# The roll layer's last four images in two groups of two, without filler products

## The reference

```python
def _L1_attn_ref(x, W_A, W_V, W_O, b_O):
    z = jnp.einsum('bse,he->bsh', x, W_A) * SCALING
    z = jax.nn.softmax(z, axis=1)
    zp = jnp.transpose(z, (0, 2, 1))
    ...
    idx = (i - j) % S
    tril = (j <= i).astype(x.dtype)
    roll = zp[:, :, idx] * tril
    v = jnp.einsum('bse,fe->bsf', x, W_V).reshape(B, S, H, D)
    out = jnp.einsum('bhij,bjhd->bihd', roll, v).reshape(B, S, E)
    return jnp.einsum('bse,fe->bsf', out, W_O) + b_O
...
h = h + _L1_attn_ref(_layernorm(h, axis=-1), ...)
h = h + _L1_ffn_ref(_layernorm(h, axis=-1), ...)
```

## Time and profile before

| What | Value |
|---|---|
| median of 3 runs | 1072.96 us (1072.81 to 1073.27) |
| the profiled execution | 1074.8 us, its span 1073.0 us |
| mean granted TensorE clock over the span | 0.936 |
| PE busy | 939.0 us, 88% of the span |
| DVE, ACT, POOL busy | 582.3, 412.1, 519.4 us |
| roll layer, its steps 7 and 8 | from 806.4 to 850.8 us, 22.2 us each |
| roll layer, its steps 9 and 10 | from 850.8 us to DVE's last instruction at 874.8 us |

### The profile page before, as it was taken

The page is one execution under the profiler, slowest core; times in us unless marked ns, Lnnn a source line. Parts: engine busy times, 40 slices in busy tenths (PEclk is TensorE's granted clock), DMA queues, the critical chain, the costliest instruction groups (busy, mean ns, idle before and its releaser), DMA issues. The chain is left out here.

```text
span 1073.0 us, 29482 instructions
## 1 busy us (share of the span) xinstructions
PE 939.0 (88%) x10318; PEld 741.5 (69%) x10318; DVE 582.3 (54%) x1439; ACT 412.1 (38%) x1094; POOL 519.4 (48%) x714
## 2 busy tenths in 40 slices
PE   8699999978824999999999986599999954999996
PEld 6457777767722888888888875255665634888895
DVE  1768888855995677533333325678877432111111
ACT  2357667743334343443434311233333222333331
POOL 0045565620603777777677617777772002343332
PEclk9879999979967999999999989789999976999998
DMA  7010000002003988887888723335463047466750
GB/s 253 2 44 2 0 0 0 1 2 84 1 0 109 307 267 271 279 243 214 254 261 253 231 80 103 103 104 140 122 214 125 21 153 261 138 224 236 282 154 25
DMA packets 79820, 149.28 MB, mean 139 GB/s; under 512 B 18892, under 2 KB 53327, under 8 KB 75760
## 3 DMA queue, kind: packets, MB, share of 16 engines
q1 hardware_dynamic: 34768, 77.15, 21.4%
q0 software_dynamic: 17712, 47.88, 15.7%
q10 hardware_dynamic: 27248, 23.09, 6.4%
HBM read 200.22 MB, written 31.73 MB: 216 GB/s over the span
## 5 line engine op out<-in xcount | busy, mean ns | idle before, releaser
L1311 POOL DMA_INDIRECT x_x<-m_x_rows,x_idx x170 | 165.8, 975 | 75.2 <-issue 35.9
L1337 PE MATMUL x_pup<-x_xt,x_w 128*128 128x128 f32 (+1 forms) x2176 | 184.7, 251 | 0.0
L1337 PEld LDWEIGHTS x_pup<-x_xt,x_w 128*128 128x128 f32 (+1 forms) x2176 | 168.7, 166 | 6.0 <-issue 5.9
L1606 POOL DMA_INDIRECT rl_y<-m_y_rows,rl_idx x136 | 132.8, 976 | 46.3 <-issue 36.9
L1407 DVE TENSOR_TENSOR x_hid<-x_gate,x_pup 128x128 f32<-128x128 f32 x170 | 48.9, 288 | 148.3 <-ACT x_gate L1379 144.3
L1351 PE MATMUL x_pdown<-x_w,x_hid 128*128 128x256 f32 (+1 forms) x408 | 104.2, 389 | 0.3 <-DVE x_y L1414 0.3
L1375 ACT ACTIVATE x_xt<-x_pturn 128x256 f32<-128x256 f32 x170 | 65.3, 384 | 88.9 <-PE x_pturn L1322 86.0
L434 POOL TENSOR_TENSOR wa_probs<-wa_probs,wa_peak 68x544 f32<-68x544 f32 x64 | 69.9, 1092 | 58.7 <-DVE wa_peak L576 58.7
L2365 DVE TENSOR_TENSOR x_y<-x_pdown,x_b 128x256 f32<-128x256 f32 x21 | 8.9, 425 | 151.3 <-PE x_pdown L2321 151.3
L2351 ACT ACTIVATE x_hid<-x_pup,x_b 128x128 f32<-128x128 f32 (+1 forms) x200 | 52.9, 356 | 93.3 <-PE x_pup L2304 93.1
L1379 ACT ACTIVATE x_gate<-x_pup 128x128 f32<-128x128 f32 x170 | 47.2, 278 | 93.5 <-PE x_pup L1337 92.8
(11 more groups left out here) (329 smaller groups left out, 1886.8 us busy)
## 6 DMA issues: line engine op xcount, KB each, us to landing
x_w<-in_experts SPq DMA_DIRECT2D x204, 384.0 KB
late_w<-in_w SPq DMA_DIRECT2D x28, 1024.0 KB, 14.5
m_y_rows<-x_y ACTq DMA_DIRECT2D x170, 128.0 KB
xT<-in_w SPq DMA_DIRECT2D x12, 1024.0 KB, 6.2
xn<-in_w SPq DMA_DIRECT2D x10, 1024.0 KB, 10.7
h<-in_w SPq DMA_DIRECT2D x10, 1024.0 KB, 14.7
m_x_rows<-xn SPq DMA_DIRECT2D x34, 128.0 KB, 1.9
x_x<-m_x_rows,x_idx POOLq DMA_INDIRECT x170, 3.1
```

The costliest lines, as they stand in the source:

```text
L1311: nc.gpsimd.indirect_dma_start(x[:, s, :], None, x_rows, bass.IndirectOffsetOnAxis(ap=idx[:, s:s + 1], axis=0))\
L1337: mm = nc.tensor.matmul(pup[rows:rows + wide, bank, m * P + side * wide:m * P + (side + 1) * wide], w[:, lane, first:first + wide], xt[:, ...
L1606: nc.gpsimd.indirect_dma_start(y[:, t % YR, kk, :], None, y_rows, bass.IndirectOffsetOnAxis(ap=idx[:, n:n + 1], axis=0))\
```

## The change

The list `SIZES` replaces the constant number of groups: seven groups of four images and two of two. The pipeline has one step more (12 instead of 11). Tile 15 becomes the end of group 7 and tile 16 that of group 8; the out part of group 6 has tiles 12 and 13, that of group 7 tile 14, that of group 8 tiles 15 and 16. No group projects more than two tiles any more, so `project` and `add_projected` run once a group. The instructions of a group of two have half the columns or half the count. The three filler helpers return at once, without their waits, for groups 7 and 8 (the last two, as g1 in steps 8 and 9). The fillers of the closing branch stay: eight ahead of the inverse, and three behind it. Since NG is now 9, SP's four weight loads stand ahead of the rows of group 5 instead of group 4.

```diff
-    NG = B // GI
+    GI, PAIR = 4, 2
+    SIZES = [4] * 7 + [2] * 2
+    NG = len(SIZES)
+    FROM = [sum(SIZES[:g]) for g in range(NG + 1)]
...
-        return list(range(0 if g == 0 else 2 * g + 1, 2 * g + 3))
+        return list(range(-(-FROM[g] * S // P), -(-FROM[g + 1] * S // P)))
...
-        return list(range(2 * g, NT if g == NG - 1 else 2 * g + 2))
...
+        return list(range(FROM[g] * S // P, FROM[g + 1] * S // P))
+
+    def halves(g):
+        return range(SIZES[g] // PAIR)
...
-                        mm = nc.tensor.matmul(pz[0:H, 0:GC], late["w_a"][:, c, :], xT[:, c, g * GC:(g + 1) * GC],
+                        mm = nc.tensor.matmul(pz[0:H, 0:SIZES[g] * S], late["w_a"][:, c, :], xT[:, c, cols_of(g)],
...
                 def fill(g, n):
+                    if NG - 2 <= g < NG:
+                        return
...
                 def fill_values(g, n):
-                    pe.wait_ge(v_moved, g * 2 + 2)
+                    if NG - 2 <= g < NG:
+                        return
+                    pe.wait_ge(v_moved, pairs_through(g))
...
                 def fill_mid(g, n):
-                    if not 0 <= g < NG:
+                    if not 0 <= g < NG - 2:
                         return fill(g, n)
...
                         fill(g2 + 1, 8)
-                        invert(g2, 0)
-                        fill(g2 + 1, 4)
-                        invert(g2, 1)
-                        fill(g2 + 1, 2)
-                        for m, ts in pairs_out(g2):
-                            project(g2, m, ts)
+                        for p in halves(g2):
+                            invert(g2, p)
+                            fill(g2 + 1, 3)
+                        project(g2)
...
                     if has1:
-                        values(g1, 1)
+                        for p in halves(g1)[1:]:
+                            values(g1, p)
```

More of the change, by code:

```diff
@@ L1476, in roll_layer @@
     inv = [k["const"]("inv_re"), k["const"]("inv_neg"), k["const"]("inv_im"), k["const"]("inv_im")]
-    GI = 4
-    NG = B // GI
+    GI, PAIR = 4, 2
+    SIZES = [4] * 7 + [2] * 2
+    assert sum(SIZES) == B
+    NG = len(SIZES)
+    FROM = [sum(SIZES[:g]) for g in range(NG + 1)]
     GC = GI * S
-    CP = 2 * S
+    CP = PAIR * S
     YR = 4
@@ L1490, in tiles_out, with pair_of, pairs_through, cols_of @@
             return []
-        return list(range(2 * g, NT if g == NG - 1 else 2 * g + 2))
-    def pairs_out(g):
-        ts = tiles_out(g)
-        return [(ts[n] // 2, ts[n:n + 2]) for n in range(0, len(ts), 2)]
+        return list(range(FROM[g] * S // P, FROM[g + 1] * S // P))
+    def halves(g):
+        return range(SIZES[g] // PAIR)
+    def pair_of(g, p):
+        return FROM[g] // PAIR + p
+    def pairs_through(g):
+        return FROM[g + 1] // PAIR
+    def cols_of(g):
+        return slice(FROM[g] * S, FROM[g + 1] * S)
+    assert all(len(tiles_out(g)) <= 2 for g in range(NG))
     STEPS = NG + 3
@@ L1641, in forward @@
                 def forward(g, p, part):
-                    n = (g * 2 + p) * 2 + part
-                    pe.wait_ge(v_moved, g * 2 + p + 1)
+                    n = pair_of(g, p) * 2 + part
+                    pe.wait_ge(v_moved, pair_of(g, p) + 1)
                     if n >= 3:
@@ L1650, in turn_mix @@
                     pe.wait_ge(z_normed, g + 1)
-                    for b in range(GI):
+                    for b in range(SIZES[g]):
                         mm = nc.tensor.transpose(pz[0:S, b * H:(b + 1) * H], z[:, b, :], ident[0:H, 0:H])
@@ L1657, in forward_mix @@
                     for part in range(2):
-                        mm = nc.tensor.matmul(pz[0:NF, (1 + part) * GI * H:(2 + part) * GI * H], fwd[part],
-                                              zt[:, :, :].rearrange("s b m -> s (b m)"), start=True, stop=True)
+                        at = (1 + part) * GI * H
+                        mm = nc.tensor.matmul(pz[0:NF, at:at + SIZES[g] * H], fwd[part],
+                                              zt[:, 0:SIZES[g], :].rearrange("s b m -> s (b m)"), start=True, stop=True)
                     mm.then_inc(zf_done, 1)
                 def invert(g, p):
-                    j = g * 2 + p
+                    j = pair_of(g, p)
                     pe.wait_ge(terms, (j + 1) * 4)
@@ L1675, in invert, with project @@
                     mm.then_inc(inverted, 1)
[L1677 to L1681, removed]
+                def project(g):
+                    pe.wait_ge(out_moved, pairs_through(g))
+                    if g:
+                        pe.wait_ge(proj_added, g)
+                    for s, t in enumerate(tiles_out(g)):
                         nc.tensor.matmul(pr[:, s, :], ident, late["b_o"][:, :], start=True, stop=False)
@@ L1748, in _ @@
                         forward(g2, 0, 1)
-                        forward(g2, 1, 0)
+                        for p in halves(g2)[1:]:
+                            forward(g2, p, 0)
                     for t in tiles_in(g1):
@@ L1787, in _ @@
                     if has2:
-                        invert(g2, 1)
-                        fill_values(g1, 2)
+                        for p in halves(g2)[1:]:
+                            invert(g2, p)
+                            fill_values(g1, 2)
                     if has1:
                         turn_mix(g1)
-                    for m, ts in pairs_out(g2):
-                        project(g2, m, ts)
+                    if has2:
+                        project(g2)
                     if has1:
@@ L1874, in _ @@
                     if has2 and not has1:
-                        move_out(g2, 0)
-                        move_out(g2, 1)
+                        for p in halves(g2):
+                            move_out(g2, p)
                         root("out", outs)
@@ L1895, in _ @@
                     if has1:
-                        move_values(g1, 1)
+                        for p in halves(g1)[1:]:
+                            move_values(g1, p)
                         exp(g1)
                     if has2:
-                        move_out(g2, 0)
-                        move_out(g2, 1)
+                        for p in halves(g2):
+                            move_out(g2, p)
                     if has1:
@@ L2003, in _ @@
                         continue
+                    if outs:
+                        dve.wait_ge(proj_added, g3 + 1)
                     for t in outs:
-                        dve.wait_ge(proj_added, t // 2 + 1)
                         measure("out", t)
@@ L2019, in _ @@
                     if has2:
-                        multiply(g2, 1)
+                        for p in halves(g2)[1:]:
+                            multiply(g2, p)
                     if has1:
```

57 lines of the change are left out of this document (33 added, 24 removed).

## The result

The changed kernel takes **1083.16 us** (median of 3 runs, 1082.48 to 1083.17) against 1072.96 before: ratio 1.0092, 95% interval 1.0077 to 1.0107. It is slower by 0.9%, outside the predicted range of 1072.0 to 1079.0. The profiled execution took 1082.48 us with a span of 1080.7, which is 7.7 longer than the span before. The loss in it is 8.36 us. Ahead of it the profiled execution after was 1.72 us shorter than that before, and behind it 1.06 longer; that makes the 7.7 of the spans.

What follows compares the result with a forecast made beforehand. PE's chain of products paces the layer's end: 17.1 + 13.5 + 6.4 + 8.65 = 45.65 us against 46.23 (-0.6), plus 2.7 for one clock fall in step 9, gives +2.1: 1075.1 us, range 1072.0 to 1079.0.

Steps and rivals of the forecast that it cites:

- step 8: Step with a group of two as g1: 17.1 us at full clock against 22.19 before, so 5.1 won.
- Step 9: The added step: 13.5 us at full clock, with PE lacking real work for most of 4.2 us before its inverse.
- The closing step: Last step up to its projection, now with one pair: 6.4 us against 10.93.
- The tail: From the last projection to DVE's last start: 8.65 us against 13.11, without the wait for a third tile's turn.
- The loads: SP's four weight loads, issued a step later, near 814 us: claimed to cost nothing.
- the 2.3 us stretch: In step 8, 6.67 to 8.97 us after its start, without fillers: the clock was expected to hold there.
- the second rival: The clock falls in step 8 as well as step 9: +5 us, 1078 us; chance 0.14.
- lower bound of 0.6 us: Smallest price of step 9's clock fall, if the clock only falls within the inverse or comes back during it.
- upper bound of 4.8: Largest price of step 9's clock fall in us, if the clock stays low until the closing step's fillers.
- the forecast's case: One clock fall, in step 9, costing 2.7 us, so +2.1 us in all; range 1073.0 to 1077.2 us.
- the section of the Trainium skill that I cited: "HAM oscillation" section: bursts shorter than their waits each start at low clock; by it step 8 would pay too.
- The rival of overlap: Engines overlap more in step 9, which falls below 12 us: -2.1 us or more, about 1070.5 us; chance 0.08.

Runs made afterwards that it cites:

- e7: Changed kernel with fillers restored in steps 8 and 9 only beside the turns and behind an inverse (eight and six): 1074.35 us, ratio 1.0013.
- e10: Changed kernel with only the fillers behind an inverse restored, four in step 8 and two in step 9: 1080.68 us, ratio 1.0067.
- e3: Changed kernel with all fillers back in step 8, none in step 9: 1078.82 us, ratio 1.0052 to the kernel before.
- e8: Changed kernel with only the fillers beside the turns restored, four each in steps 8 and 9: 1081.72 us, ratio 1.0076.
- e2: Kernel before, old groups, with the fillers of step 8 alone taken out: 1075.40 us, ratio 1.0012.
- e6: Kernel before, old groups, with fillers ahead of the first inverse, half between inverses and those behind projection and mixture removed in all steps: 1070.07 us, ratio 0.9964.
- e4: Changed kernel with all fillers back in step 9, none in step 8: 1080.40 us, ratio 1.0062 to the kernel before.

## Why the prediction was wrong

**Where it held.** By the rows of after, each piece of PE's work put at its full-clock length (that of e7's row for the same piece), step 8 is 21.78 - 4.52 = 17.26 us: 1.77 from the second inverse, 2.58 from its projection and 0.17 from the mixture's transform (17.1 predicted). Step 9 is 15.29 - 2.14 = 13.15 (13.5): the first turn out starts 6.0 after the step's start (6.1), the second 7.5 (8.0), the inverse 8.9 (9.35). The closing step is 6.45, by e7's (6.4). The tail is 8.68 (8.65). The sum is 45.54, predicted 45.65, against 46.23 before. e7, at full clock with fillers that cost next to nothing, confirms it from the other side: 0.42 us below before where I had 0.6. The loads were issued from 812.13 on (near 814 predicted); no compute engine waited for a transfer between 826.87 and 872, and the sum leaves nothing for them.

**What failed** is one sentence: "I take it that the clock (2.4 GHz) falls to 1.2 GHz in the second and not in the first." It fell in both. The reason I gave, that dense work stands on both sides of the 2.3 us stretch, is what the runs refute: the work behind it is the inverse, 64 matmuls of 68 rows by 64 columns. PE counts as busy for the whole of 836 to 838 in after, and the clock falls right behind it; e10 shows the same even with two fillers put there. What happened is the second rival, to which I gave 0.14, but not at its price.

**The price was too low as well.** I took "some 6 us at 0.50" from one case in the earlier trace rows, where PE came back to turns, fillers and the logits. Here the clock stayed low for 10.24 us each time. Step 9's fall came 1.3 us inside its inverse, where I had a lower bound of 0.6 us, and still reached into the closing step. By the rows above, the first fall cost 4.52 us, the second 2.14 in step 9 and 2.39 in the closing step: 4.53, near the upper bound of 4.8. So 9.05 together, where the forecast had 2.7 for one and the rival some 5.6 for two. In e3, where the stretch was 6.83 us, the same fall cost about 2.5 (15.33 - 13.15 in step 9 and 0.36 behind it): the forecast's price, and the forecast's case. PE came back to the same inverse there, so the work alone doesn't explain 6.83 or 10.24; what does stays open. -0.7 + 9.05 is the 8.36 of the profile. The medians differ by 10.2 and the profiled executions by 7.7: that of before lay 1.84 above its median, that of after 0.68 below.

The Trainium skill, page "TensorE: Matmul & The Clock Gate", section "A second HAM failure mode: psum-queue depth-cycling", describes a clock that oscillates because PE idles briefly and often between groups of products, not once for long. That is nearer to these traces than the section of the Trainium skill that I cited, which tells of waits longer than the bursts of work between them: no wait of PE in step 8 of after was longer than 0.59 us, and the clock fell. The fall at 874.4, with PE busy for 1.65 of the 2 us ahead of it, is no case of such waits either. So I was wrong to read the section I cited as speaking for a fall in step 8, and I didn't weigh the nearer one.

**The rival of overlap** (1070.5 us) is out: step 9 is 13.15 at full clock, not under 12.

## What to carry to other kernels

Ask of a filler two things apart: whether it lies in a wait (then it is free) or on PE's path (then it costs its length), and whether the clock holds without it. Here about half of them were on the path and could go, the other half held the clock, and taking out either part of that half let it fall, at some 4 us a time (8.78 us for two falls in e8, 8.03 in e10, each against e7). A stretch that PE is "busy" for with small products wasn't cover here; price a fall by the longest low stretch that a trace shows and by the work that lies in it, and allow for one in each step that lacks fillers.

## What the hardware showed that I had not expected

- A stretch of small products at a busy share of 100% neither kept the clock nor brought it back: in after step 8's second inverse ran 3.89 us at 0.50, and the clock returned only 5.6 us after the projection had started (842.98 to 848.6, products of 128 rows by 128 columns nearly throughout).
- In e10 the clock fell in a window (838 to 840) in which PE was counted busy for 2.00 of 2.00 us. In step 8 it lacks against e7, which held the clock, only the fillers beside the turns, and those stand ahead of the first inverse. So the place where a fall shows needn't be the place that lacks work.
- A fall lasted 6.83 us in e2, e3, e6 and the second time in e10, and 10.24 us in after, e4, e8 and the first time in e10: by e3 and after, that is a price of 2.5 or 4.5 us for the same missing products of step 9.
